# The causal mask of a decoder layer's attention: from a TensorE product to an addition on VectorE

## The chip, the cores and the metric

The kernel runs on one core of a Trainium2 chip. The metric is device time in microseconds (us); before the change it is 997.43 us, the median of three runs (995.61 to 999.0). The core has five engines that work side by side and meet only through semaphores: TensorE (PE in the profile, its weight loads PEld), VectorE (DVE), ScalarE (ACT), GpSimd (POOL) and SyncE (SP), which issues the DMAs.

## The reference

A decoder layer on 8 sequences of 256 tokens with 512 features: causal self-attention (16 heads of 32 features, 4 key heads), causal cross-attention to a context, and a feed-forward part, each with a residual and a layer norm. The part that matters is the same in both attentions:

```python
att = jnp.einsum('bhqd,bhkd->bhqk', q, k) * scale
causal = jnp.tril(jnp.ones((T, T), dtype=bool))
att = jnp.where(causal[None, None], att, -jnp.inf)
att = jax.nn.softmax(att, axis=-1)
y = jnp.einsum('bhqk,bhkd->bhqd', att, v)
```

## The kernel before

The attentions fill the first 525 us or so of the span; after them come the preparation of the feed-forward weights and the feed-forward part, which the change does not touch. The attentions are 16 **turns** (8 sequences of self-attention, then 8 of cross-attention), a turn has four **steps**, and a step handles one group of four heads. So there are 64 groups. A group's scores lie in three PSUM banks, its **units**: A (bank 0) has the first 128 queries against the first 128 keys for four heads, B and C (banks 1 and 2) have the last 128 queries against all 256 keys for two heads each.

Each step overlaps three groups. TensorE (`scores`, `transposes`, `outputs`) computes the scores of group i, transposes the probabilities of group i-1, multiplies those of group i-2 with the values, and then does one to three **fillers**: projections for this and the next turn (`sv`, `sq`, `sk` in self-attention, `cv`, `cq`, `ck`, `x1t` in cross-attention, `wo` and `wout` for the output). VectorE (`step` in its body) takes the maxima of group i (`maxima`), copies two transposed tiles of group i-1 with the reciprocals and the output of group i-2 between them (`probT_tile`, `reciprocals`, `output`), and then does its share of the fillers: the low halves of projections (`lo`, L710), or residual, statistics and normalisation (L777 to L787). ScalarE (`step` in its body) copies the first transposed tile (L668), does the exponentials of the three units with their sums (L678), and then its share of the fillers (L629, L633).

The order on each engine is written out by hand. What ties the engines together: TensorE may write unit u of the next group only when ScalarE has finished the exponentials of that unit (s_exp), the exponentials of a unit wait for its maxima (s_max), and the fillers alternate between banks 3 and 4, so that each filler on TensorE waits until the one before the last has been drained by VectorE or ScalarE.

The mask before: ahead of the scores of a unit, TensorE multiplies a 128x128 identity with a bf16 tile of zeros and -1e30 (L893 for unit A, 512 columns; L898 for B and C, 256 columns), which opens the accumulation in the bank; the score products then add to it. VectorE reads the bank once with one max-reduction for each unit (L736), negated.

Of the kernel before, what the change touches and what calls it, by code (L numbers as in the profile page):

```python
# [26 lines left out]
BF16 = mybir.dt.bfloat16  # L27
ALU = mybir.AluOpType
ACT = mybir.ActivationFunctionType
AX = mybir.AxisListType  # L30
# [305 lines left out]
def attention_phase(nc, ctx, sb, sem, A, banks, x2, ident, s_const, s_passed):  # L336
# [27 lines left out]
    mv = sb(ctx, "mv", [P, TT, 2])  # L364
    rstd = sb(ctx, "rstd", [P, TT, 2])
    half = sb(ctx, "half", [P, 1])
    ident16 = sb(ctx, "ident16", [P, P], BF16)
    mask16 = sb(ctx, "mask16", [P, HG, P], BF16)
    W_RING = 4
    wraw = sb(ctx, "wraw", [P, W_RING, D])  # L370

# [76 lines left out]
    with nc.Block() as block:  # L448
# [92 lines left out]
        @block.gpsimd  # L541
        def _(g):
            g.memset(ident[:, :], 0.0).then_inc(s_const, 1)
            g.memset(ident16[:, :], 0.0).then_inc(s_const, 1)
            g.memset(mask16[:, :, :], 0.0).then_inc(s_const, 1)
            g.memset(half[:, :], -0.5).then_inc(s_const, 1)
            g.wait_ge(s_const, 4)
            for m in (ident, ident16):
                g.affine_select(out=m[:, :], in_=m[:, :], compare_op=ALU.not_equal, fill=1.0, base=0,
                                pattern=[[-1, P]], channel_multiplier=1).then_inc(s_const, 1)  # L550

            g.affine_select(out=mask16[:, :, :], in_=mask16[:, :, :], compare_op=ALU.is_ge, fill=MASKED, base=0,
                            pattern=[[0, HG], [-1, P]], channel_multiplier=1).then_inc(s_const, 1)

            def split(hi, lo, raw, s_h, s_l, n):
                g.tensor_scalar(hi, raw, 1.0, 1.0, ALU.mult, ALU.mult).then_inc(s_h, 1)
# [54 lines left out]
        def _(s):  # L611
# [51 lines left out]
            def body(t):  # L663
                def step(i):
                    if t.turned(i):
                        s.wait_ge(s_T, t.groups(i - 2, U, 1))
                        bank = banks[T_BANKS[(U * (i - 1)) % 2]]
                        s.activation(probT[:, (i - 1) % 2, :, 0:P], bank[:, :].rearrange("p (j q) -> p j q", j=HG), ACT.Copy).then_inc(s_cpA, 1)  # L668
                    if not t.scored(i):
                        return  # L670
                    for u in range(U):
                        if u and t.turned(i):
                            s.wait_ge(s_T, t.groups(i - 2, U, u + 1))
                        s.wait_ge(s_max, t.groups(i - 1, U, u + 1))
                        heads = range(HG) if u == 0 else range(2 * (u - 1), 2 * u)
                        width, qt = (P, 0) if u == 0 else (S, 1)
                        for c, j in enumerate(heads):
                            ins = s.activation(prob[:, u, c * width:(c + 1) * width], banks[u][:, c * width:(c + 1) * width], ACT.Exp,  # L678
                                               bias=nmax[:, i % 2, qt, j:j + 1], accum_out=den[:, i % 2, qt, j:j + 1])
                        ins.then_inc(s_exp, 1)  # L680

                for i in range(t.steps()):
                    step(i)
                    weights(*split_at(t, i, True))
                    for name in t.fillers(i):
                        projection(t, name)
                    if t is first_cross and i == 2:
                        pr.wait_full(s, t, ("wo", TT - 1))
                    weights(*split_at(t, i, False))
# [4 lines left out]
        def _(v):  # L694
# [35 lines left out]

            def body(t):
                def maxima(i, u):
                    v.wait_ge(s_S, t.groups(i - 1, U, u + 1))
                    width, qt = (P, 0) if u == 0 else (S, 1)
                    heads = slice(0, HG) if u == 0 else slice(2 * (u - 1), 2 * u)
                    v.tensor_reduce(nmax[:, i % 2, qt, heads], banks[u][:, :].rearrange("p (j k) -> p j k", k=width), AX.X, ALU.max, negate=True).then_inc(s_max, 1)  # L736

                def probT_tile(i, u):
                    v.wait_ge(s_T, t.groups(i - 1, U, u + 1))
# [68 lines left out]
        def _(t_):  # L808
# [62 lines left out]
                t_.wait_ge(s_wlo, KEYS if name[0] == "sk" else QUERIES)  # L871
                projection(pro, name)
            t_.wait_ge(s_wlo, VALUES)
            t_.wait_ge(s_const, 7)

            def body(t):
                def scores(i):
# [10 lines left out]
                    for u in range(U):  # L888
                        bank = banks[u]
                        if t.turned(i):  # L890
                            t_.wait_ge(s_exp, t.groups(i - 2, U, u + 1))
                        if u == 0:
                            t_.matmul(bank[:, :].rearrange("p (j k) -> p j k", j=HG), ident16[:, :], mask16[:, :, :], start=True, stop=False, skip_group_check=True)  # L893
                            for j in range(HG):
                                ins = t_.matmul(bank[:, j * P:(j + 1) * P], qh[:, j, 0:P], kh[:, j, 0:P], start=False, stop=j == HG - 1, skip_group_check=True)  # L895
                        else:
                            diag = bank[:, :].rearrange("p (j c k) -> p j c k", j=2, c=2)[:, :, 1, :]
                            t_.matmul(diag, ident16[:, :], mask16[:, 0:2, :], start=True, stop=False, skip_group_check=True)  # L898
                            for c in (0, 1):
                                j = 2 * (u - 1) + c  # L900
                                ins = t_.matmul(bank[:, c * S:(c + 1) * S], qh[:, j, P:S], kh[:, j, :], start=False, stop=c == 1, skip_group_check=True)
                        ins.then_inc(s_S, 1)

                def transposes(i, u):
# [754 lines left out]
```

## Time and profile before

| what | value |
|---|---|
| median of 3 runs | 997.43 us |
| the profiled execution, its own time | 1000.47 us |
| its span | 998.7 us |
| PE, DVE, ACT, POOL busy | 914.9, 682.4, 526.4, 431.6 us |
| mean granted TensorE clock | 0.971 of full speed |
| chain that ended last | PE 25% of the span, DVE 5%, issue 1% |

An engine's busy time is an average over stages with different limits, and busy PE is not PE at its peak, since its instructions overlap. The time of a turn is read from the stretches between the first weight load of one turn's scores and that of the next.

### The profile page before, as it was taken

To read this page: it belongs to the slowest core of one execution; us is meant where nothing else is said; L and a number is where in the kernel's file an instruction comes from. 1 tells how busy PE (TensorE), PEld (TensorE's weight loads), DVE (VectorE), ACT (ScalarE), POOL (GpSimd) and SP (SyncE) were. 2 spreads that over 40 slices of the span, in tenths; PEclk is the share of its full clock that TensorE was granted. 3 is DMA by queue.
4 is the path that set the end of the run, shared out by engine and by line. 5 is a ranking of instruction groups with operands and counts; after the bars stand their busy time and mean duration, and the time that the engine had idled before them with its cause. 6 is when DMAs were issued, how large, how long until landed. Compare 5 with 4: busy or idle time off the path is not lost. (4 is left out here: it accounts for less than half of the span.)

```text
span 998.7 us, 19666 instructions
## 1 busy us (share of the span) xinstructions
PE 914.9 (92%) x6030; PEld 757.6 (76%) x6092; DVE 682.4 (68%) x1240; ACT 526.4 (53%) x1640; POOL 431.6 (43%) x603
## 2 busy tenths in 40 slices
PE   4899999999988999999995897989999999999993
PEld 4788888888767888888884665667778778778773
DVE  3667766777767777777774688693657657657466
ACT  3656555565557556766561433435564564564461
POOL 0233233342222222322222587970565565566466
PEclk8999999999999999999997898999999999999998
DMA  5313322334445535354420765541101101000001
GB/s 164 125 66 122 106 79 89 105 105 152 118 132 144 136 82 141 111 137 106 109 80 0 236 223 196 190 147 64 43 1 43 42 0 42 0 0 35 8 1 42
DMA packets 67043, 92.96 MB, mean 93 GB/s; under 512 B 7217, under 2 KB 41009, under 8 KB 66609
## 3 DMA queue, kind: packets, MB, share of 16 engines
q1 hardware_dynamic: 66992, 92.34, 29.8%
q8 instruction: 25, 0.41, 0.2%
q14 instruction: 26, 0.20, 0.1%
HBM read 39.89 MB, written 4.19 MB: 44 GB/s over the span
## 5 line engine op out<-in xcount | busy, mean ns | idle before, releaser
L678 ACT ACTIVATE prob<-bank,nmax 128x128 f32<-128x128 f32 (+1 forms) x512 | 207.0, 435 | 18.1 <-DVE nmax L736 17.7
L161 PE MATMUL bank<-w_ffn,hT 128*128 128x512 f32 x768 | 193.1, 403 | 0.0
L161 PEld LDWEIGHTS bank<-w_ffn,hT 128*128 128x128 f32 x768 | 141.6, 190 | 31.1 <-POOL hT L1372 0.2
L566 POOL TENSOR_SCALAR rwide<-rden 128x256 f32<-128x256 f32 x64 | 26.0, 406 | 255.7 <-DVE rden L745 255.7
L161 PE MATMUL bank<-xT,w_att 128*128 128x256 f32 x864 | 119.2, 290 | 12.8 <-DVE w_att L702 10.1
L736 DVE TENSOR_REDUCE nmax<-bank 128x2 f32<-128x512 f32 (+1 forms) x192 | 120.7, 683 | 13.7 <-PE bank L895 13.7
L161 PEld LDWEIGHTS bank<-xT,w_att 128*128 128x128 f32 x864 | 113.3, 196 | 16.5 <-DVE xT L725 7.3
L161 PE MATMUL bank<-tile 128*128 128x512 f32 x384 | 100.4, 416 | 19.8 <-DVE tile L1183 19.8
L678 ACT ACTIVATION_READ_ACCUMULATOR prob<-bank,nmax 128x1 f32 x512 | 113.9, 223 | 0.0
L913 PE MATMUL bank<-ident,prob 128*128 128x128 f32 x768 | 105.9, 274 | 0.8 <-ACT prob L678 0.4
L1444 ACT ACTIVATE ht<-bank,cols 128x128 f32<-128x128 f32 x192 | 72.2, 457 | 64.4 <-PE bank L1581 64.4
L161 PEld LDWEIGHTS bank<-tile 128*128 128x128 f32 x384 | 73.3, 197 | 42.5 <-DVE tile L1183 18.5
L161 PE MATMUL bank<-w_att,oT 128*128 128x512 f32 x384 | 97.7, 405 | 2.6 <-POOL oT L558 2.5
L913 PEld LDWEIGHTS bank<-ident,prob 128*128 128x128 f32 x768 | 88.5, 142 | 1.3 <-ACT prob L678 0.6
L161 PE MATMUL bank<-x2T,w_ffn 128*128 128x512 f32 x384 | 88.5, 391 | 1.0 <-POOLq L113 1.0
L1501 DVE TENSOR_TENSOR y<-bank,stage_bias 128x512 f32<-128x512 f32 x64 | 44.1, 690 | 64.1 <-PE bank L161 64.1
L741 DVE COPY probT<-bank 128x512 f32<-128x512 f32 x128 | 87.2, 681 | 1.1 <-PE bank L913 1.1
L161 PEld LDWEIGHTS bank<-x2T,w_ffn 128*128 128x128 f32 x384 | 72.0, 188 | 16.9 <-POOLq L113 1.4
L161 PEld LDWEIGHTS bank<-w_att,oT 128*128 128x128 f32 x384 | 71.6, 193 | 17.3 <-issue 3.2
L1372 POOL TENSOR_TENSOR hT<-ht,hT 128x512 fp32r<-128x512 f32 x48 | 67.2, 1399 | 38.1 <-ACT hT L1449 38.0
L668 ACT ACTIVATE probT<-bank 128x512 f32<-128x512 f32 x64 | 38.2, 597 | 85.7 <-PE bank L913 85.7
L1183 DVE TENSOR_TENSOR tile<-raw,tile 128x1024 fp32r<-128x1024 f32 x32 | 51.6, 1622 | 21.0 <-ACT tile L1100 20.7
(125 smaller groups left out, 1557.7 us busy)
## 6 DMA issues: line engine op xcount, KB each, us to landing
q<-stage SPq DMA_DIRECT2D x192, 128.0 KB, 2.3
k<-kstage SPq DMA_DIRECT2D x48, 256.0 KB, 3.6
raw<-in_ent_wT SPq DMA_DIRECT2D x32, 256.0 KB, 3.2
raw<-in_ent_pw SPq DMA_DIRECT2D x32, 256.0 KB, 3.7
xT_raw<-in_xT SPq DMA_DIRECT2D x8, 512.0 KB, 4.4
xres<-in_x SPq DMA_DIRECT2D x8, 512.0 KB, 3.6
xb<-x SPq DMA_DIRECT2D x8, 512.0 KB, 4.4
aux<-in_path_w SPq DMA_DIRECT2D x8, 512.0 KB, 3.5
```

The lines of the kernel that those rows point to most:

```text
L161: ins = t.matmul(out, lhs(a, k), rhs(b, k), start=first and n == 0 and m == 0, stop=last and n == len(kts) - 1 and m == 2, skip_group_chec ...
L566: g.tensor_scalar(rwide[:, i % 2, :, :].rearrange("p t (j d) -> p t j d", j=HG), src, 1.0, 1.0, ALU.mult, ALU.mult).then_inc(s_wide, 1)
L668: s.activation(probT[:, (i - 1) % 2, :, 0:P], bank[:, :].rearrange("p (j q) -> p j q", j=HG), ACT.Copy).then_inc(s_cpA, 1)
L678: ins = s.activation(prob[:, u, c * width:(c + 1) * width], banks[u][:, c * width:(c + 1) * width], ACT.Exp, bias=nmax[:, i % 2, qt, j:j + ...
L736: v.tensor_reduce(nmax[:, i % 2, qt, heads], banks[u][:, :].rearrange("p (j k) -> p j k", k=width), AX.X, ALU.max, negate=True).then_inc(s ...
L741: v.tensor_copy(probT[:, i % 2, 2 * (u - 1):2 * u, P:PW], bank[:, :].rearrange("p (j q) -> p j q", j=2)).then_inc(s_cpB, 1)
L913: ins = t_.transpose(bank[:, c * P:(c + 1) * P], prob[:, u, c * P:(c + 1) * P], ident[:, :])
L1183: v.tensor_tensor(tile[:, kt % HR, 1, :, :], raw[:, kt % R, :, :], tile[:, kt % HR, 0, :, :].bitcast(F32), ALU.subtract).then_inc(s_lo, 1)
L1372: g.tensor_tensor(hT[:, 1, :, i * P:(i + 1) * P], ht[:, u % HT, :, :], hT[:, 0, :, i * P:(i + 1) * P].bitcast(F32), ALU.subtract).then_inc ...
L1444: ins = s.activation(ht[:, u % HT, c, :], bank[:, c * P:(c + 1) * P], ACT.Identity, bias=shift(u // BT, c), scale=gain(u // BT, c))
L1501: k.drain(("mm", u), v.tensor_tensor(y[:, i, :], banks[plan.bank(("mm", u))][:, :], bias[:, s_, :], ALU.add))
```

## The change

TensorE no longer multiplies the mask; the first score product of a unit opens the accumulation. VectorE adds the mask while it looks for the maxima: `tensor_tensor_reduce` reads a head's scores from the bank and the mask from SBUF (a tile of 128x256 floats: zeros for the first 128 keys, the triangle for the last), writes the negated sum back in place, and keeps the minimum of what it wrote as the bias of the exponential. ScalarE then takes the exponential with scale -1. One instruction handles one head of 128 or 256 keys, where one max-reduction handled a whole unit of 512 columns. The wait ahead of each unit is now an instruction of its own (`wait_alone`).

```diff
@@ VectorE
                 def maxima(i, u):
-                    v.wait_ge(s_S, t.groups(i - 1, U, u + 1))
+                    wait_alone(v, s_S, t.groups(i - 1, U, u + 1), s_passed)
                     width, qt = (P, 0) if u == 0 else (S, 1)
-                    heads = slice(0, HG) if u == 0 else slice(2 * (u - 1), 2 * u)
-                    v.tensor_reduce(nmax[:, i % 2, qt, heads], banks[u][:, :].rearrange("p (j k) -> p j k", k=width), AX.X, ALU.max, negate=True).then_inc(s_max, 1)
+                    for c, j in enumerate(range(HG) if u == 0 else range(2 * (u - 1), 2 * u)):
+                        scored = banks[u][:, c * width:(c + 1) * width]
+                        ins = v.tensor_tensor_reduce(scored, scored, mask[:, S - width:S], scale=-1.0, scalar=3e38, op0=ALU.add, op1=ALU.min,
+                                                     accum_out=nmax[:, i % 2, qt, j:j + 1])
+                    ins.then_inc(s_max, 1)
@@ ScalarE
-                                               bias=nmax[:, i % 2, qt, j:j + 1], accum_out=den[:, i % 2, qt, j:j + 1])
+                                               scale=-1.0, bias=nmax[:, i % 2, qt, j:j + 1], accum_out=den[:, i % 2, qt, j:j + 1])
@@ TensorE
-                        if u == 0:
-                            t_.matmul(bank[:, :].rearrange("p (j k) -> p j k", j=HG), ident16[:, :], mask16[:, :, :], start=True, stop=False, skip_group_check=True)
-                            for j in range(HG):
-                                ins = t_.matmul(bank[:, j * P:(j + 1) * P], qh[:, j, 0:P], kh[:, j, 0:P], start=False, stop=j == HG - 1, skip_group_check=True)
-                        else:
-                            diag = bank[:, :].rearrange("p (j c k) -> p j c k", j=2, c=2)[:, :, 1, :]
-                            t_.matmul(diag, ident16[:, :], mask16[:, 0:2, :], start=True, stop=False, skip_group_check=True)
-                            for c in (0, 1):
-                                j = 2 * (u - 1) + c
-                                ins = t_.matmul(bank[:, c * S:(c + 1) * S], qh[:, j, P:S], kh[:, j, :], start=False, stop=c == 1, skip_group_check=True)
+                        width, at = (P, 0) if u == 0 else (S, P)
+                        heads = list(range(HG) if u == 0 else range(2 * (u - 1), 2 * u))
+                        for c, j in enumerate(heads):
+                            ins = t_.matmul(bank[:, c * width:(c + 1) * width], qh[:, j, at:at + P], kh[:, j, 0:width], start=c == 0, stop=c == len(heads) - 1, skip_group_check=True)
...
```

On GpSimd two small tiles of constants are no longer made before the first scores.

TensorE, the scores of one group before (bank0 is unit A, bank1 and bank2 are B and C; k3 and q3 are the stacked keys and queries):

```order
L893 MATMUL bank0<-mask16,ident16 128x512 [waits s_exp,s_qst2]
L895 MATMUL bank0<-k3,q3 128x128 x4
L898 MATMUL bank1<-mask16,ident16 128x2x128 [waits s_exp]
L901 MATMUL bank1<-k3,q3 128x256 x2
L898 MATMUL bank2<-mask16,ident16 128x2x128 [waits s_exp]
L901 MATMUL bank2<-k3,q3 128x256 x2
```

TensorE, the same place after the change:

```order
L895 MATMUL bank0<-k3,q3 128x128 [waits s_exp,s_qst2]
L895 MATMUL bank0<-k3,q3 128x128 x3
L895 MATMUL bank1<-k3,q3 128x256 [waits s_exp]
L895 MATMUL bank1<-k3,q3 128x256
L895 MATMUL bank2<-k3,q3 128x256 [waits s_exp]
L895 MATMUL bank2<-k3,q3 128x256
```

The three mask products are gone, and the waits stand at the first score product of each unit; nothing else moves.

VectorE, from the last filler of one self-attention step to the first copy of the next, before:

```order
L710 SCALAR_TENSOR_TENSOR stage<-bank4,stage 128x256 [waits s1_hi]
L733 REGISTER_ALU
L736 TENSOR_REDUCE nmax<-bank0 128x4 [waits s_S]
L733 REGISTER_ALU
L736 TENSOR_REDUCE nmax<-bank1 128x2 [waits s_S]
L733 REGISTER_ALU
L736 TENSOR_REDUCE nmax<-bank2 128x2 [waits s_S]
L741 COPY probT<-bank6 128x2x256 [waits s_T]
```

VectorE, the beginning of the same place after the change, units A and B (an ISA row that names a bank is the new operation, the ISA row with nmax alone behind it reads out the minimum that it kept):

```order
L707 SCALAR_TENSOR_TENSOR stage<-bank4,stage 128x256 [waits s1_hi]
L152 REGISTER_ALU
L734 ISA bank0,nmax<-bank0,mask 128x128 [waits s_S]
L734 ISA nmax 128x1
L734 ISA bank0,nmax<-bank0,mask 128x128
L734 ISA nmax 128x1
L734 ISA bank0,nmax<-bank0,mask 128x128
L734 ISA nmax 128x1
L734 ISA bank0,nmax<-bank0,mask 128x128
L734 ISA nmax 128x1
L152 REGISTER_ALU
L734 ISA bank1,nmax<-bank1,mask 128x256 [waits s_S]
```

Where three instructions stood for a group, sixteen stand now: eight that work on a head and eight that read out a minimum. Everything behind them on VectorE keeps its place.

## Rows read from the trace of the kernel before

**Rows 1.** Windows: a self-attention turn, the passage to cross-attention, a cross-attention turn
```profile
core 0: us, PE busy (x) PEld busy (x) DVE busy (x) ACT busy (x) POOL busy (x), PEclk, DMA share, GB/s
143.61:174.27 30.66, 30.66 (x270) 27.04 (x273) 21.79 (x46) 17.62 (x75) 11.17 (x18) 1.00 0.28 98
242.13:316.00 73.87, 65.62 (x530) 55.20 (x538) 54.66 (x107) 45.23 (x167) 18.14 (x37) 0.98 0.55 151
404.25:436.11 31.86, 30.70 (x260) 26.27 (x263) 24.01 (x49) 20.05 (x78) 8.86 (x18) 1.00 0.44 119
```

**Rows 2.** Timeline of TensorE's weight loads, a self step: start, length, operation
```profile
153.91 1.42 PEld L161 LDWEIGHTS bank<-w_att,xT 128*128 128x128 f32 x12
155.25 1.50 PEld L161 LDWEIGHTS bank<-xT,w_att 128*128 128x128 f32 x12
156.79 0.10 PEld L893 LDWEIGHTS bank<-mask,ident 128*128 128x128 bf16 x1
...
157.42 0.10 PEld L898 LDWEIGHTS bank<-mask,ident 128*128 128x128 bf16 x1
...
157.78 0.10 PEld L898 LDWEIGHTS bank<-mask,ident 128*128 128x128 bf16 x1
```

**Rows 3.** Groups of VectorE by line and shape: busy us, mean ns, idle before
```profile
L736 DVE TENSOR_REDUCE nmax<-bank 128x2 f32<-128x512 f32 x128 | 82.1, 682 | 0.0
L755 DVE TENSOR_TENSOR o<-bank,rT 128x256 f32<-128x256 f32 x64 | 27.2, 424 | 3.3
```

**Rows 4.** Timeline of VectorE in step 0 of a self turn
```profile
176.50 1.89 DVE L736 TENSOR_REDUCE nmax<-bank 128x4 f32<-128x512 f32 x3
```

**Rows 5.** Timeline of ScalarE in the same step
```profile
177.23 0.37 ACT L678 ACTIVATE prob<-bank,nmax 128x128 f32<-128x128 f32 x1 [0.37 <-DVE nmax L736]
...
177.59 0.36 ACT L678 ACTIVATE prob<-bank,nmax 128x128 f32<-128x128 f32 x1
...
179.51 0.50 ACT L678 ACTIVATE prob<-bank,nmax 128x256 f32<-128x256 f32 x1
...
179.96 0.51 ACT L678 ACTIVATE prob<-bank,nmax 128x256 f32<-128x256 f32 x1
180.32 0.24 ACT L678 ACTIVATION_READ_ACCUMULATOR prob<-bank,nmax 128x1 f32 x1
```

**Rows 6.** Timeline of weight loads: unit C of the step behind it
```profile
181.86 0.10 PEld L898 LDWEIGHTS bank<-mask,ident 128*128 128x128 bf16 x1
```

**Rows 7.** Waits of the cross turn 404.25 to 436.11: total us, times, longest
```profile
PEld bank L866 <- DVE stage L710: 1.0, 1, 1.0
...
PEld bank L161 <- ACT cv L633: 0.6, 1, 0.6
```

**Rows 8.** Timeline of VectorE in that cross turn, steps 0 and 2
```profile
406.20 1.88 DVE L736 TENSOR_REDUCE nmax<-bank 128x4 f32<-128x512 f32 x3
...
420.11 1.88 DVE L736 TENSOR_REDUCE nmax<-bank 128x4 f32<-128x512 f32 x3
...
422.50 0.19 DVE L745 RECIPROCAL rden<-den 128x8 f32<-128x8 f32 x1
422.61 0.37 DVE L751 COPY rT<-bank 128x256 f32<-128x256 f32 x1
...
423.36 0.68 DVE L741 COPY probT<-bank 128x512 f32<-128x512 f32 x1
424.99 0.69 DVE L710 SCALAR_TENSOR_TENSOR kstage<-bank,kstage 128x512 fp32r<-128x512 f32 x1 [0.95 <-ACT kstage L629]
```

**Rows 9.** Timeline of ScalarE in step 0 of that turn
```profile
406.92 0.37 ACT L678 ACTIVATE prob<-bank,nmax 128x128 f32<-128x128 f32 x1
...
410.09 0.64 ACT L633 ACTIVATE cv<-bank 128x512 f32<-128x512 f32 x1
```

**Rows 10.** Timeline of weight loads in that turn, steps 0 and 2
```profile
410.78 0.53 PEld L161 LDWEIGHTS bank<-w_att,ctxT 128*128 128x128 f32 x3 [0.62 <-ACT cv L633]
...
425.74 1.61 PEld L161 LDWEIGHTS bank<-xT,w_att 128*128 128x128 f32 x12
```

More of the change, by code:

```diff
@@ L366, in attention_phase @@
     half = sb(ctx, "half", [P, 1])
-    ident16 = sb(ctx, "ident16", [P, P], BF16)
-    mask16 = sb(ctx, "mask16", [P, HG, P], BF16)
+    mask = sb(ctx, "mask", [P, S])
     W_RING = 4
@@ L543, in _ @@
             g.memset(ident[:, :], 0.0).then_inc(s_const, 1)
-            g.memset(ident16[:, :], 0.0).then_inc(s_const, 1)
-            g.memset(mask16[:, :, :], 0.0).then_inc(s_const, 1)
+            g.memset(mask[:, :], 0.0).then_inc(s_const, 1)
             g.memset(half[:, :], -0.5).then_inc(s_const, 1)
[L547 to L553, printed above, removed]
+            g.wait_ge(s_const, 3)
+            g.affine_select(out=ident[:, :], in_=ident[:, :], compare_op=ALU.not_equal, fill=1.0, base=0,
+                            pattern=[[-1, P]], channel_multiplier=1).then_inc(s_const, 1)
+            g.affine_select(out=mask[:, P:S], in_=mask[:, P:S], compare_op=ALU.is_ge, fill=MASKED, base=0,
+                            pattern=[[-1, P]], channel_multiplier=1).then_inc(s_const, 1)
             def split(hi, lo, raw, s_h, s_l, n):
@@ L873, in _ @@
             t_.wait_ge(s_wlo, VALUES)
-            t_.wait_ge(s_const, 7)
+            t_.wait_ge(s_const, 5)
             def body(t):
```

## The prediction

> **What bounds the kernel now.** I read the busy shares first: PE 92% of the span, DVE 68%. That average hides what matters here, so next I cut the attentions into turns with the windows view. In a self-attention turn TensorE is busy in all of its 30.66 us, and VectorE in 21.79 [rows 1]. In a cross-attention turn TensorE has 30.70 us of work in 31.86, VectorE 24.01 [rows 1]. So self-attention goes by TensorE's work, and in cross-attention TensorE already waits. The waits of the cross turn say for whom: once for VectorE's low half of a projection, once for ScalarE's copy of cv, 1.0 and 0.6 us [rows 7]. Both stand at the end of the same chain: scores, maxima on VectorE, exponentials on ScalarE, the fillers' copies, TensorE's next filler. Then the timelines of single steps, to see where that chain is tight.
>
> **What TensorE saves.** The mask products are overlapped with loads, so I take spacings and not lengths. From the mask's weight load of unit B to that of unit C is 157.42 to 157.78, 0.36 us, for a mask product and two score products of 256 columns [rows 2]. Twelve products of that width in the filler take 155.25 to 156.79, 0.128 each, so two take 0.257, and the mask costs 0.10. Unit A takes 156.79 to 157.42, 0.63; four products of 128 columns cost four times (155.25 - 153.91) / 12 = 0.112, so 0.45, and the mask 0.18. A group saves 0.18 + 0.10 + 0.10 = 0.39 us (rounded up), a turn 1.56, all 64 groups 25 us. That is the whole possible gain, if nothing else becomes late.
>
> **What VectorE pays.** Removed: three reductions of 512 columns, 682 ns long [rows 3], but overlapping: three take 1.89 [rows 4], so one starts 0.605 after the other and 0.077 of each length is hidden. VectorE is held 1.8 us. Added: four instructions on 128 and four on 256 columns, and behind each a read-out. The trace has no such instruction, and none in which VectorE writes a bank.
> - The nearest row of the work itself: two tensors, one from a bank, 256 columns, 424 ns [rows 3]. The slope between it and the 512-column reduction is 258 ns for 256 columns, so 128 columns are 295 ns long. With 0.077 hidden: 0.218 and 0.347 apart.
> - The nearest row of a read-out: a reciprocal of 8 elements holds the engine 0.11 (422.50 to 422.61) [rows 8]. Then the group costs 4 x 0.328 + 4 x 0.457 = 3.14 us.
> - The nearest row of such a pair is ScalarE's exponential with its sum: pairs start 0.36 apart at 128 columns, 0.45 at 256 [rows 5]. Stretched to VectorE's slope (1.01 ns a column against (450 - 360) / 128 = 0.70) that is 0.40 and 0.53, 3.7 us a group; unstretched it is 3.24.
> - Lower end: the read-outs hide entirely, 2.26. Upper end: nothing overlaps and a read-out is 0.19 long, 4 x 0.485 + 4 x 0.614 = 4.40; if reading and writing one bank also halved the rate, 3.14 + 0.13 x 4 + 0.26 x 4 = 4.70.
>
> I take 3.3, near the first two prices: +1.5 us of VectorE for each group. Unit A, which ScalarE waits for first, is ready 1.44 us after the start in place of 0.68, B and C follow 0.97 us apart, faster than the exponentials of a unit need (four at 0.36), so only A delays them: 0.76 us.
>
> The Trainium skill, "Vector Engine (DVE) Microarchitecture Reference", section "Measured stream behaviour on trn2", gives 1.04 ns a column and about 75 ns fixed for each instruction, programs of several micro-operations included. An estimate from that page would be 0.21 and 0.34 for the work and 0.08 for a read-out, 2.8 us a group. The trace agrees on the slope (1.01) and the fixed part (0.605 - 0.516 = 0.09) for built-in operations; for this one it shows nothing. This speaks for the first rival below.
>
> **What it does in self-attention.** VectorE's 21.79 us become 27.8, below TensorE's new 29.1, so the sum does not decide, the order in the step does. In step 0 VectorE comes late to the maxima, since it first normalises for the turn before: it starts at 176.50 [rows 4], and ScalarE already waits for it 0.37 [rows 5]. That start hangs on VectorE's own work in step 3 and stays. The exponentials start 0.76 later, at 177.99, and end at 180.32 + 0.24 + 0.76 = 181.32. TensorE needs that for unit C of the next group, now at 181.86 [rows 6]; by its own work it will be there 0.39 (step before) + 0.39 + 0.28 (masks of A and B) = 1.06 earlier, 180.80. So it waits 0.5. The other three steps start their maxima early enough, or are long enough (two hold an output projection); I allow another 0.2. A turn: -1.56 + 0.7 = -0.86.
>
> **In cross-attention.** Step 0: maxima at 406.20 [rows 8], exponentials at 406.92, the copy of cv at 410.09 [rows 9], for which TensorE waits until 410.78 [rows 10]. The exponentials come 0.76 later and so does everything in this chain; TensorE's saving lies inside its wait. Since the fillers ahead end up to 0.15 earlier, I count +0.6. Step 1: its maxima wait for the scores, which come sooner; -0.1. Step 2: maxima at 420.11; the group holds VectorE 3.3, then the copies, reciprocal and output 423.96 - 421.90 = 2.06 (423.36 + 0.68 - 0.08 is their end [rows 8], 420.11 + 1.79 their start). So it is free at 425.5 for the low half of kstage, which now starts at 424.99 [rows 8]; TensorE's next filler, now just in time at 425.74 [rows 10], comes 0.5 later. Step 3 is hardly touched. A turn: +1.0.
>
> **Elsewhere.** The passage between the attentions (242 to 316) has VectorE at 54.66 of 73.87 us with the splitting of the cross weights [rows 1]; ten groups there bring it 15 us more. Where it is the one waited for (I count three steps) that is +1.5 each, less 0.39 in the seven others: +2. The constants on GpSimd and the sign of the exponential cost nothing: they lie beside DMAs, or are a field of the instruction.
>
> **The sum.** Seven self turns x -0.86 = -6.0; seven cross turns x +1.0 = +7.0 (one of each kind falls into the start or the passage); passage +2. Together +3. On the profiled execution, 1000.47, that is 1003.5. This execution stands 3.04 above the median of the runs, so 1000.5.
>
> **Rivals.**
> 1. TensorE's gain wins. If the group costs VectorE 2.8, A is ready 1.2 after the start: the exponentials are 0.5 later. Self turns then lose only some 0.4 of their 1.56 (-1.2, seven: -8.4), cross turns are about even (+0.1), the passage 0: -8, 989. At 2.26 it would be -20 (978). For it: TensorE's full 30.66 of 30.66. Against: VectorE's late start in step 0. Chance 0.30.
> 2. VectorE becomes the bound of both attentions. From about 3.9 us a group its work, 21.79 - 3 x 4 x 0.68 + 4 x 3.9 = 29.2, passes TensorE's 29.1 in self turns. At 4.4 it has 31.2 us and the 1.3 us or so of waits that stay: 32.5, +1.9 a turn; in cross turns 24.01 - 8.2 + 17.6 + 1.3 = 34.7, +2.9; with +8 in the passage +42, 1039. At 4.7 it would be 1055. The place is the same maxima, the price the pair of instructions. For it: ScalarE's pairs, stretched, give 3.7. Against: every VectorE row that follows another overlaps it. Chance 0.20, of which half beyond 1030.
> 3. The change does not free TensorE: the mask's products might fill time in which the stacked keys' loads could not run anyway. Then the spacings stay, and only VectorE's lateness is left: +15, 1012. The 0.36 against 0.257 speaks against it. Chance 0.05.
>
> My forecast (3.1 to 3.7 us a group) has 0.45, and its own range is 994 to 1015: above 3.3 each 0.1 us a group is worth about 3.5 us over the groups, in late maxima and late fillers, below it less, since TensorE's own work takes over.
>
> **Chances.** What a measurement can tell from no change is 0.3%, 3 us: below 994.4 is faster, above 1000.4 slower. Faster: rival 1 nearly whole, 0.27, and 0.02 of the forecast. Same: 0.23 of the forecast and 0.03 of rival 1. Slower: 0.20 of the forecast, rivals 2 and 3: 0.45. The range 984 to 1032 leaves out what lies beyond 2.5 us and 4.2 us a group.
>
> **What will show it.** TensorE: no rows with mask; the spacing of unit B 0.26 in place of 0.36, unit A 0.45. VectorE: 512 new instructions with 512 read-outs; from the first of a group to the copy behind it 3.3 us (2.8 for rival 1, over 3.9 for rival 2). Self turns 29.8 us long, with waits of TensorE for ScalarE's exponentials of some 0.5 in step 0; cross turns 32.9, with the waits for cv and kstage grown. The prediction is wrong if VectorE's rows come out under 3 or over 3.7 us a group, or if VectorE starts its maxima of step 0 earlier than now, so that self turns keep the whole 1.56.

## The result

| kernel | median of runs, us | lowest to highest | against before |
|---|---|---|---|
| before (4 runs of the same chip) | 998.11 | 995.61 to 999.0 | 1 |
| after (4 runs) | 987.66 | 985.95 to 989.78 | 0.990, 95% interval 0.987 to 0.9931 |

The change makes the kernel 1.0% faster. The forecast was 1000.5 us, no change or a little slower. The profiled execution of after took 986.26 us, its span 984.4.

**Where the time went.** Each group has one reciprocal on VectorE, 64 in all. I cut both traces at the 5th, 29th, 37th and 61st: six self turns, the passage, six cross turns (all groups of the same kind in both). Windows of before, columns as in [rows 1]:

```profile
61.67:247.81 186.14, 186.14 (x1631) 164.45 (x1654) 131.38 (x273) 107.09 (x456) 67.00 (x108) 1.00 0.31 103
247.81:319.21 71.40, 63.15 (x509) 52.73 (x516) 53.63 (x106) 43.88 (x163) 17.76 (x36) 0.98 0.52 142
319.21:510.41 191.20, 184.23 (x1549) 157.63 (x1574) 144.03 (x290) 120.29 (x470) 53.12 (x108) 1.00 0.43 116
```

The same windows of after:

```profile
59.67:235.85 176.18, 176.12 (x1578) 156.77 (x1578) 146.46 (x585) 107.27 (x453) 67.00 (x108) 1.00 0.33 109
235.85:308.27 72.42, 60.08 (x477) 50.47 (x479) 58.98 (x210) 43.71 (x162) 17.75 (x36) 0.96 0.49 138
308.27:498.50 190.23, 177.48 (x1522) 151.81 (x1515) 160.22 (x601) 122.12 (x474) 53.19 (x108) 1.00 0.44 117
```

Self-attention gives 9.96 us (1.66 a turn, all that TensorE saves); the passage takes 1.02 back; cross-attention gives only 0.97 (0.16 a turn). What is left of the 14.3 us between the two spans lies ahead of the 5th reciprocal (2.0) and between the 61st and the last (0.8), where seven changed groups stand, and behind the attentions (1.6), in code that the change does not touch; the runs of one kernel spread by 2 to 6 us. In the passage the granted clock is also lower, 0.96 against 0.98.

**What the group costs.** VectorE in step 0 of a self turn of after, against [rows 4]:

```profile
167.80 0.30 DVE L734 CUSTOM_DVE_ANT_0 bank<-bank,mask 128x128 f32<-128x128 f32 x1
168.01 0.14 DVE L734 DVE_READ_ACCUMULATOR2_ANT nmax<- 128x1 f32 x1
168.01 0.33 DVE L734 CUSTOM_DVE_ANT_0 bank<-bank,mask 128x128 f32<-128x128 f32 x1
168.26 0.14 DVE L734 DVE_READ_ACCUMULATOR2_ANT nmax<- 128x1 f32 x1
...
169.14 0.14 DVE L734 DVE_READ_ACCUMULATOR2_ANT nmax<- 128x1 f32 x1
169.14 0.46 DVE L734 CUSTOM_DVE_ANT_0 bank<-bank,mask 128x256 f32<-128x256 f32 x1
169.52 0.14 DVE L734 DVE_READ_ACCUMULATOR2_ANT nmax<- 128x1 f32 x1
...
170.29 0.68 DVE L741 COPY probT<-bank 128x512 f32<-128x512 f32 x1
```

A read-out has the same start as the next head's work: 140 ns long, it costs little. The first head's work, with no read-out beside it, is followed after 0.21 us, the next ones after 0.25: 0.04 for the read-out. So heads start 0.25 apart at 128 columns and 0.38 at 256, and the copy behind the group starts 170.29 - 167.80 = 2.49 us after its first instruction. So the group costs 2.5 us, not 3.3. ScalarE's first exponential of that step:

```profile
168.93 0.37 ACT L675 ACTIVATE prob<-bank,nmax 128x128 f32<-128x128 f32 x1 [1.40 <-DVE nmax L734]
```

That is 1.13 after the maxima's start, against 177.23 - 176.50 = 0.73 before [rows 4, 5]: A is 0.40 later, not 0.76. Among the groups of VectorE by line and shape, as in [rows 3], the read-outs are:

```profile
L734 DVE DVE_READ_ACCUMULATOR2_ANT nmax<- 128x1 f32 x512 | 71.5, 140 | 0.0
```

They are 71.5 us in the sum, and at 0.04 each some 20 us of VectorE's time: the busy time of overlapping instructions is no price.

**TensorE.** The scores of one self step, weight loads of after, against [rows 2]:

```profile
157.69 1.00 PEld L895 LDWEIGHTS bank<-k,q 96*128 96x128 f32 x8
158.63 0.47 PEld L907 LDWEIGHTS bank<-ident,prob 128*128 128x128 f32 x4
```

0.94 us from the first load to the load behind the segment. The whole self turn shrinks by 1.66, 0.41 a group; 0.39 was forecast.

**Waits.** TensorE's and ScalarE's waits in the cross window 319.21 to 510.41 of before (total us, times, longest):

```profile
PEld bank L866 <- DVE stage L710: 5.9, 6, 1.0
...
PEld bank L161 <- ACT cv L633: 3.7, 6, 0.6
...
ACT prob L678 <- DVE nmax L736: 2.1, 6, 0.4
```

and in the window 308.27 to 498.50 of after:

```profile
ACT prob L675 <- DVE nmax L734: 12.6, 18, 0.9
...
PEld bank L161 <- ACT cv L630: 8.9, 6, 1.5
...
PEld bank L866 <- DVE stage L707: 5.7, 6, 1.0
...
PEld bank L161 <- DVE kstage L707: 3.4, 6, 0.6
```

TensorE waits 18.0 us instead of 9.6. Of the 6 x 1.66 = 10.0 us that it saves in six turns, 8.4 come back as waits: 5.2 more for ScalarE's copy of cv, 3.4 for VectorE's low half of kstage, 0.2 less for stage. That is where the gain of cross-attention went. The rest of the window agrees: 191.20 - 10.0 + 8.4 = 189.6, measured 190.23.

Not all of it is VectorE's price. The same cross window of the kernel without any mask, whose VectorE does what it did before (experiment 1), has

```profile
PEld bank L161 <- ACT cv L633: 6.4, 6, 1.1
PEld bank L866 <- DVE stage L710: 5.6, 6, 1.0
...
PEld bank L161 <- DVE kstage L710: 0.5, 3, 0.2
```

so 2.9 of the 8.4 us come back only because TensorE is sooner at copies that are not, and 5.5 by VectorE's longer group (cv 2.5, kstage 2.9).

### The profile page after: what moved, and what is told of

Its sections match the earlier page's. It is cut to its first block and busy times, and to the rows that moved or that the text cites. A ratio compares the mean times of both kernels' runs of the same rounds, so it can differ in the third digit from the quotient of the medians.

```text
span 984.4 us, 20365 instructions
## 1 busy us (share of the span) xinstructions
PE 891.6 (91%) x5900; PEld 739.3 (75%) x5900; DVE 724.3 (74%) x2072; ACT 528.6 (54%) x1640; POOL 430.6 (44%) x601
## 5 line engine op out<-in xcount | busy, mean ns | idle before, releaser
L734 DVE CUSTOM_DVE_ANT_0 bank<-bank,mask 128x128 f32<-128x128 f32 (+1 forms) x512 | 164.1, 392 | 10.8 <-PE bank L895 10.5
L161 PE MATMUL bank<-xT,w_att 128*128 128x256 f32 x864 | 120.8, 293 | 15.4 <-DVE w_att L699 10.5
L675 ACT ACTIVATION_READ_ACCUMULATOR prob<-bank,nmax 128x1 f32 x512 | 111.6, 218 | 0.0
L1438 ACT ACTIVATE ht<-bank,cols 128x128 f32<-128x128 f32 x192 | 72.3, 457 | 64.2 <-PE bank L1575 64.2
L895 PE MATMUL bank<-k,q 96*128 96x128 f32 (+1 forms) x512 | 73.5, 286 | 5.1 <-DMA q<-stage 3.4
L895 PEld LDWEIGHTS bank<-k,q 96*128 96x128 f32 x512 | 66.3, 196 | 8.0 <-DVE w_att L699 2.5
```

Of the source, the lines that this page charges most:

```text
L161: ins = t.matmul(out, lhs(a, k), rhs(b, k), start=first and n == 0 and m == 0, stop=last and n == len(kts) - 1 and m == 2, skip_group_chec ...
L734: ins = v.tensor_tensor_reduce(scored, scored, mask[:, S - width:S], scale=-1.0, scalar=3e38, op0=ALU.add, op1=ALU.min, accum_out=nmax[:, ...
L895: ins = t_.matmul(bank[:, c * width:(c + 1) * width], qh[:, j, at:at + P], kh[:, j, 0:width], start=c == 0, stop=c == len(heads) - 1, skip ...
L1438: ins = s.activation(ht[:, u % HT, c, :], bank[:, c * P:(c + 1) * P], ACT.Identity, bias=shift(u // BT, c), scale=gain(u // BT, c))
```

## The experiments

The kernel before took 998.2 us beside experiments 1 to 3, 997.9 beside 4, 6 and 7, and 997.2 beside 5, 8 and 9; differences from before are taken from these. "Group" is the spacing from the first instruction of a group's maxima to the copy behind it; the windows are those between the same reciprocals.

| kernel | group, us | time, us | ratio to before, 95% | self turn | passage | cross turn |
|---|---|---|---|---|---|---|
| before | 1.80 | 998 | 1 | 31.02 | 71.4 | 31.87 |
| no mask at all | 1.80 | 978.9 | 0.9795 to 0.9836 | 29.27 | 71.0 | 30.64 |
| one instruction a unit | 1.90 | 981.0 | 0.9823 to 0.9853 | 29.27 | 72.3 | 30.94 |
| A stays on TensorE | 2.1 | 989.8 | 0.990 to 0.993 | 30.23 | 71.9 | 31.40 |
| after | 2.49 | 987.7 | 0.987 to 0.9931 | 29.36 | 72.4 | 31.71 |
| mask on both engines | 2.49 | 1005.4 | 1.0041 to 1.0085 | 31.08 | 72.6 | 32.44 |
| 0.8 us idle work behind C | 3.3 | 1005.1 | 1.0064 to 1.0099 | 30.02 | 74.7 | 32.39 |
| 0.8 us idle work, spread | 3.2 | 1002.9 | 1.0024 to 1.006 | 30.10 | 76.8 | 32.57 |
| 0.8 us idle work ahead of A | 3.3 | 1021.1 | 1.0213 to 1.0257 | 30.46 | 78.9 | 34.78 |
| one small copy a head | 2.7 | 1018.2 | 1.0195 to 1.0233 | 31.09 | 74.3 | 34.12 |
| two small copies a head | 3.3 | 1034.6 | 1.0352 to 1.039 | 32.46 | 76.9 | 35.20 |
| normalisation later | 2.5 | 983.8 | 0.9843 to 0.9872 | 29.31 | 71.9 | 31.51 |
| one instruction a unit, normalisation later | 1.9 | 975.8 | 0.9766 to 0.9805 | 29.29 | 70.9 | 30.56 |

**1. TensorE's gain by itself.** The kernel before, without any mask (it leaves the causal mask out):

```diff
-                            t_.matmul(bank[:, :].rearrange(...), ident16[:, :], mask16[:, :, :], start=True, ...)
                             ...
-                                ins = t_.matmul(bank[:, j * P:(j + 1) * P], ..., start=False, ...)
+                            ins = t_.matmul(bank[:, c * width:(c + 1) * width], ..., start=c == 0, ...)
```

> The kernel before without the mask products on TensorE; VectorE keeps its three max-reductions for a group, so the attention is not causal here. It gives TensorE's saving alone. By my theory (the mask's products cost TensorE 0.39 to 0.43 us a group; VectorE's later maxima gave part of it back in the changed kernel) self turns come to 30.66 - 4 x 0.42 = 29.0 us, cross turns, bound by the chain through the exponentials, to some 31.0; the time is 16 to 22 us under the kernel before, 976 to 982, and 6 to 12 under the changed kernel. By the rival theory (VectorE's dearer maxima cost nothing at all, the whole change is TensorE's saving) it equals the changed kernel, 987 to 988.

Measured 978.9 us (978.07 to 981.66), 19.3 under before. That is what TensorE's saving is worth while VectorE does what it did: 1.75 us a self turn, 1.23 a cross turn. The passage, with eight groups, gains only 0.4 (its granted clock is 0.95 here). So cross turns and passage give part of the saving back before VectorE does anything more. Rival 3 falls.

**2. VectorE's price by itself.** The changed kernel, and TensorE does its mask products too (the mask is applied twice):

> The changed kernel with TensorE's mask products put back: VectorE adds the mask a second time in place and takes the minima head by head. It gives VectorE's price alone: 0.7 us more of VectorE for a group, unit A ready some 0.45 us later. My theory: the self turns have slack and stay within 0.2 us of 30.66 (a wait for the exponentials of unit C just begins to show), the cross turns become 0.6 to 1.0 us longer (32.5 to 32.9), together +5 to +10 us, 1003 to 1008. Rival (VectorE's lateness is hidden everywhere): within 0.3% of the kernel before.

Measured 1005.42 us (1000.87 to 1006.73), 7.2 over before and 17.8 over after. In the profile most of it is in cross-attention (+0.57 a turn) and the passage (+1.2); a self turn does not see it (+0.06). The two parts nearly add up, -19.3 + 7.2 = -12.1, measured -10.5. VectorE's price is higher once TensorE is quick: a cross turn pays 0.57 here, and 31.71 - 30.64 = 1.07 with the mask off TensorE.

**3. One and two more small operations a head.**

```diff
                     for c, j in enumerate(...):
+                        v.tensor_copy(idle[:, 4 * u + c:4 * u + c + 1], half[:, :])
+                        v.tensor_copy(idle[:, ...], half[:, :])     # the second, in the second run
                         ins = v.tensor_tensor_reduce(scored, scored, mask[:, S - width:S], ...)
```

> The changed kernel with one small copy on VectorE (one column, SBUF to SBUF) ahead of each head's instruction, eight for a group. If such an operation holds VectorE 0.08 to 0.11 us, a group costs VectorE 3.2 to 3.4 us, the price that the prediction took. If only that price was wrong and the steps from it to the time were right, the time is that of the prediction: 998 to 1003. If the steps were too dark as well, it stays clearly below: 988 to 994 (self turns under 29.5 us).

> The same with two small copies ahead of each head, sixteen for a group: VectorE 3.9 to 4.3 us a group. By the prediction's second rival VectorE's work then passes TensorE's in the self turns (over 30 us) and sets both kinds of turn: 1022 to 1040. If VectorE's queue hides more than that, under 1010.

Measured 1018.23 (1014.39 to 1020.17) and 1034.63 us (1033.77 to 1035.87). The first misses both of its ranges; the second lies in its range, but not for the reason expected. A copy holds the engine 0.07 us, and part of that hides: with one a head, heads start 0.28 and 0.41 apart and the group takes 2.7 us (3.2 to 3.4 was expected), with two it takes 3.3. VectorE, with one copy, at 128 and at 256 columns:

```profile
101.95 0.15 DVE L735 COPY idle<-half 128x1 f32<-128x1 f32 x1
102.02 0.29 DVE L736 CUSTOM_DVE_ANT_0 bank<-bank,mask 128x128 f32<-128x128 f32 x1
102.23 0.14 DVE L736 DVE_READ_ACCUMULATOR2_ANT nmax<- 128x1 f32 x1
102.23 0.15 DVE L735 COPY idle<-half 128x1 f32<-128x1 f32 x1
...
103.12 0.42 DVE L736 CUSTOM_DVE_ANT_0 bank<-bank,mask 128x256 f32<-128x256 f32 x1
103.46 0.14 DVE L736 DVE_READ_ACCUMULATOR2_ANT nmax<- 128x1 f32 x1
```

With a copy between them the work alone shows: 0.21 and 0.34 us to the row behind it.

But six times VectorE stands still for 2.3 to 2.8 us with nothing to wait for, and the step there is that much longer or twice that. Each attention has a loop of three passes of two turns (eight groups). The stops lie where the second and the third pass begin, once each in self-attention and twice each in cross-attention, and none lies where the first pass begins. Two of them:

```profile
113.18 0.15 DVE L735 COPY idle<-half 128x1 f32<-128x1 f32 x1 [2.81 <-issue]
...
377.97 0.15 DVE L735 COPY idle<-half 128x1 f32<-128x1 f32 x1 [2.27 <-issue]
```

The packets of the queue that brings instructions (packets, MB, share) show something of the kind: before, after, the next kernel (three more instructions a group) and this one (eight more):

```profile
q14 instruction: 26, 0.20, 0.1%
```
```profile
q14 instruction: 29, 0.24, 0.1%
```
```profile
q14 instruction: 30, 0.25, 0.1%
```
```profile
q14 instruction: 52, 0.42, 0.1%
```

The six stops are 15.5 us, of some 31 that this kernel stands over after. The granted clock is lower too, 0.97 in the self window and 0.96 in the cross window, 1.00 in both of after. So these two runs do not measure a price of time on VectorE, and reading them needed another experiment.

**4. The same time with few instructions.** The changed kernel, and one maximum over 192 columns of the mask tile for each unit, into a cell that nobody reads:

```diff
                     width, qt = (P, 0) if u == 0 else (S, 1)
+                    v.tensor_reduce(idle[:, u:u + 1], mask[:, 0:192], AX.X, ALU.max)
```

> The changed kernel with one instruction more for each unit: VectorE takes the maximum of 192 columns of the mask tile into a cell that nobody reads (three a group, 0.27 us each by the reductions' slope, 0.258 us for 256 columns and 0.09 fixed). It adds as much time to VectorE's group (2.48 + 0.8 = 3.3 us) as the 16 small copies did, with 3 instructions in place of 16. Theory (the long steps at every second turn of the runs with small copies come from the number of VectorE's instructions in the loop body, which must be fetched again when the loop jumps back; the time per group does the rest): no step is 3 us longer than its like, the instruction queue stays near the 29 packets of the changed kernel, self turns are about 29.8 us, cross turns 32.5 to 33.9, and the time is 1000 to 1012 us. Rival (the stalls come from VectorE's time itself, at a place where the two-turn loop ends): the steps at every second turn grow by 3 us or more again, and the time is 1020 us or more, as with two copies.

Measured 1002.91 us (999.05 to 1005.33). VectorE has no such stop. The window of its passage:

```profile
243.79:320.62 76.83, 62.95 (x483) 53.18 (x483) 64.24 (x234) 43.87 (x164) 18.18 (x36) 0.91 0.45 126
```

This is nearly the kernel that the prediction described: a group of 3.2 us. It stands 5.0 us over before; the forecast was 3 over. Had the group cost what I took it to, the forecast would have been near (by terms of which two were off in opposite ways, see below). And two small copies a head, at about the same group, take 32 us more. That comes with the number of instructions, not with the time on VectorE: 15.4 us are its six stops; its granted clock is 0.96 and 0.94 in the self and cross windows against 1.00 here, and how much of the rest is the clock's no run separates.

**5. Is it A's lateness, or the sum?** The prediction said that only A delays the exponentials. Two kernels with the same three idle maxima, all ahead of A's first instruction, or all behind C's last:

```diff
+                    for n in range(U if u == 0 else 0):        # ahead of A (the other: u == U - 1, behind C)
+                        v.tensor_reduce(idle[:, ...], mask[:, 0:192], AX.X, ALU.max)
```

> The changed kernel with three maxima of 192 columns of the mask tile into unread cells, all three ahead of unit A's first instruction: 0.8 us more VectorE a group, the same as with one ahead of each unit (1002.9 us), but A is ready 1.95 us after the start in place of 1.4. Theory (the lateness of A, and with it of all exponentials, is what costs; the sum of a group counts little while VectorE has idle time in a step): self turns over 30.5 us, cross turns over 32.8, 1006 to 1015 us. Rival (the sum of VectorE's work decides): as with one ahead of each unit, 1001 to 1005.

> The same three maxima, but behind unit C's last instruction, after ScalarE has been told that the group's minima are there: A is ready after 1.13 us as in the changed kernel, and the same sum of 3.3 us comes ahead of the copies of the transposed probabilities. Theory (A's lateness costs): self turns 29.4 to 29.7, cross turns 31.9 to 32.3 because their fillers on VectorE come later too, 990 to 996 us. Rival (the sum decides): 1001 to 1005.

Measured 1021.1 us (1017.5 to 1023.91) and 1005.07 (1002.92 to 1008.04). Both lie outside the ranges of the theory, that A's lateness is what costs. The first is dearer (1006 to 1015 was expected). The second refutes it: with A as early as in after, it costs as much as the spread kernel, which the theory excluded (990 to 996). The waits in its cross window, where after has cv 8.9, stage 5.7 and kstage 3.4:

```profile
PEld bank L161 <- ACT cv L631: 8.9, 6, 1.5
...
PEld bank L869 <- DVE stage L708: 8.5, 6, 1.5
...
PEld bank L161 <- DVE kstage L708: 5.4, 6, 0.9
```

cv is untouched: what this wait gains in other kernels is A's lateness. The 4.8 us more of stage and kstage are VectorE's own fillers behind the longer group: that is the sum. In self-attention the sum counts as well, by another way. TensorE's waits for exponentials in the self windows of after, of idle work behind C and of idle work spread:

```profile
PEld bank L895 <- ACT prob L675: 0.2, 1, 0.2
```
```profile
PEld bank L898 <- ACT prob L676: 2.3, 6, 0.6
```
```profile
PEld bank L897 <- ACT prob L676: 3.4, 7, 0.6
```

Behind C the exponentials follow their maxima as in after, but VectorE comes later to the maxima of step 0, 2.7 to 3.0 us behind TensorE's first load of that group in place of 2.3 to 2.6. That wait, and 1.4 us for the copies of the transposed probabilities, make a self turn 0.66 longer than in after; with the idle work spread it is 0.74.

So there are two paths, and each has its price. Ahead of A both are paid: cv 13.6, kstage 8.1 (stage 5.7), and TensorE's granted clock falls to 0.95 in the cross window (it is 1.00 in after), which is part of the 34.78. How much of the 1021 is the clock's, no run separates.

**6. A stays where it was**, in both attentions or in cross-attention alone (`moved` says whose mask VectorE adds):

```diff
+                        moved = u > 0                       # the other: u > 0 or t.own == "self"
+                        if not moved:
+                            t_.matmul(bank[...], ident16[:, :], mask16[...], start=True, stop=False, ...)
```

> The changed kernel, but unit A's mask stays a TensorE product and its maxima one reduction of 512 columns, as before the change; units B and C are as after it. TensorE keeps 0.20 to 0.25 of its 0.43 us a group; VectorE's group is 0.6 + 4 x 0.38 = 2.1 us in place of 2.48, and A is ready 0.7 us after the start in place of 1.13, as before the change. Theory (VectorE's price that counts is how late A is ready, not the sum): cross turns fall from 31.4 to 31.0 or so, self turns rise from 29.1 to 29.8, and the time is 986 to 991 us, no better than the change in full. Rival (the sum of the group is what counts): the same saving of 0.38 in every group shows in the cross turns' steps 2 and 3, and the time falls below 984.

> The changed kernel, but in cross-attention alone unit A's mask stays on TensorE with one reduction on VectorE; self-attention is wholly as after the change. If A's lateness is what cross turns pay (they gain 0.45 us of 1.6), they fall from 31.4 to about 31.0, seven of them and the passage by about 3 us: 984 to 986 us. Rival: TensorE's own 0.2 us a step comes back onto the path in the two steps that do not wait, and the time stays at 987 to 989.

Measured 989.78 (987.76 to 991.38), in its range, and 986.18 us (984.91 to 987.96), 0.2 above its range. Cross turns are 31.40 in both, self turns 30.23 where A's product stays, much as the theory had it. But both kernels also shorten the group (to 2.1 us; the wait for kstage is gone with that for cv down to 5.1), so they do not tell A's lateness from the sum. Over after the second is 1.5 us better, which these runs do not tell from nothing (after 985.95 to 989.78). Neither is clearly better than after: leaving a part of the mask returns to TensorE what TensorE has just been relieved of.

**7. The normalisation behind the next maxima** (so that VectorE reaches them sooner):

> The changed kernel, but VectorE normalises the finished residual (L787, 3 small operations of 512 columns) behind the first maxima of the next step in place of ahead of them. If VectorE's late start in the steps behind a normalisation is what keeps the exponentials late (the wait for the maxima there is 1.4 us in self turns and 0.4 in cross turns), the exponentials come 0.4 to 0.9 us earlier in those steps, TensorE's waits for them go, and the time is 982 to 986 us. Rival: the copies of the transposed probabilities, which now stand behind the normalisation, become as late as the maxima were, and the time is 987 to 992.

Measured 983.76 us (982.59 to 987.89), 3.9 under after, with ranges that overlap. A self turn stays at 29.31, since TensorE had hardly a wait left in it (0.2 us in six turns); the cross turns lose 0.2 and the last groups 1.1. The profiled execution is the slowest of its four, 987.89, so its windows do not add up to the gain. In experiment 9, beside experiment 8, they do better: the passage loses 1.45, a cross turn 0.38, the last groups 1.1.

**8. One instruction a unit.** What costs is columns plus a fixed part for each instruction: (0.38 - 0.25) / 128 = 1.0 ns a column, and 0.25 - 0.13 = 0.12 us fixed. Eight fixed parts become three when the heads of a unit share one minimum (a softmax is the same for any shift common to its row):

```diff
-                    for c, j in enumerate(range(HG) if u == 0 else range(2 * (u - 1), 2 * u)):
-                        scored = banks[u][:, c * width:(c + 1) * width]
-                        ins = v.tensor_tensor_reduce(scored, scored, mask[:, S - width:S], ..., accum_out=nmax[:, i % 2, qt, j:j + 1])
+                    scored = banks[u][:, :].rearrange("p (j k) -> p j k", j=n)
+                    masks = mask[:, S - width:S].rearrange("p (o k) -> p o k", o=1).broadcast_to([P, n, width])
+                    v.tensor_tensor_reduce(scored, scored, masks, ..., accum_out=nmax[:, i % 2, qt, 2 * max(u - 1, 0):2 * max(u - 1, 0) + 1])
```

(ScalarE's bias names the same shared cell.)

> The changed kernel, but one instruction for a whole unit in place of one for each head: the mask tile is repeated over the heads by a stride of zero, and the heads of a unit share the minimum over all of them as their bias (the softmax is the same for any shift that is common to a row). Three instructions and three read-outs a group in place of eight and eight. From the measured spacings, 0.25 us at 128 columns and 0.38 at 256 (1.0 ns a column and 0.12 fixed), 512 columns take 0.64 us, the group 1.9 to 2.0 in place of 2.48; A is ready 0.8 us after the start in place of 1.13. TensorE keeps its whole saving. Theory (VectorE's price per group decides what is left of TensorE's saving; at 1.8 us, with the mask left out, the time was 978.9): 979 to 983 us. Rival (the repeated mask or the three-dimensional view costs the operation its rate, 0.9 us or more a unit): a group of 2.7 us or more, 990 to 996 us.

Measured 980.96 us (980.19 to 982.44). VectorE, the same place as above; the group takes 160.10 - 158.20 = 1.90:

```profile
158.20 0.69 DVE L735 CUSTOM_DVE_ANT_1 bank<-bank,mask 128x512 f32<-128x512 f32 x1
158.81 0.14 DVE L735 DVE_READ_ACCUMULATOR2_ANT nmax<- 128x1 f32 x1
...
160.10 0.69 DVE L741 COPY probT<-bank 128x512 f32<-128x512 f32 x1
```

TensorE's waits in its cross window are 13.9 us in place of after's 18.0 (cv 6.8, stage 5.7, kstage 1.4).

It keeps 16.2 of the 19.3 us that leaving the mask out gains; its waits are near those of that kernel (12.5). What it gives up: a head whose scores all lie far below those of its unit's other heads would lose its exponentials to underflow, so it is for inputs of which that can be excluded.

**9. Both.**

> One instruction a unit as in the run beside it, and VectorE normalises the finished residual behind the next step's first maxima. Alone the later normalisation gave 983.8 against 987.7 of the changed kernel. Theory (both remove the same lateness, of the exponentials in the steps behind a normalisation): together 977 to 981, less than the sum of their gains. Rival (independent): 975 to 977. If the later normalisation only moves the wait to the copies of the transposed probabilities: no better than one instruction a unit alone.

Measured 975.79 us (972.79 to 977.61), ratio 0.9786 (0.9766 to 0.9805): the best version, 21 us under before and some 12 under the change as it was made. The later normalisation gives 5.2 us here and 3.9 alone, so nothing of its gain is lost, which speaks against the theory that the two remove the same lateness.

## Why the prediction was wrong

The step that failed is one term of "What VectorE pays": the read-out. The prediction's sum was 4 x 0.328 + 4 x 0.457 = 3.14, of which eight read-outs at 0.11 are 0.88 and the work is 2.26; it then went up to 3.3 by the likeness of ScalarE's pairs. Measured: heads 0.25 and 0.38 apart, and the work alone 0.21 and 0.34 (experiment 3), so a read-out costs 0.04. The group is 2.49, nearer my lower end of 2.26 than the 3.3. The 0.11 came from a reciprocal with a copy behind it, the step up to 3.3 from another engine's read-outs. Neither is this instruction: the row nearest in what it does was not the nearest in what it costs.

- **The work itself** held: two tensors, one from a bank, written back in place, 0.21 and 0.34 against 0.218 and 0.347. Writing the bank which it reads, one reason for the upper bound, costs nothing that these rows show.
- **TensorE's saving**, 0.39 a group, held (0.41).
- **Self turns**, forecast -0.86: by the prediction's own working the exponentials end at 181.32 with a lateness of 0.76, at 180.96 with the measured 0.40, and TensorE is there at 180.80: 0.16 of wait in place of 0.5. The scores of that step do take longer than 0.94 from first load to the load behind them, in two of the six turns (1.13 and 1.19):

```profile
171.42 1.19 PEld L895 LDWEIGHTS bank<-k,q 96*128 96x128 f32 x8
172.55 0.90 PEld L907 LDWEIGHTS bank<-ident,prob 128*128 128x128 f32 x8
```

  1.13, that is 0.19 of wait. With a group of 3.2 the self turns were -0.92 against before (30.10 to 31.02), and TensorE waited for the exponentials up to 0.6 about once a turn: the place and the size held, the input was wrong. One step of the working was wrong too, that VectorE's start in step 0 "hangs on VectorE's own work in step 3 and stays". That work holds a group itself, and the start moves with it (experiment 5): 0.66 of the 0.74 us that a self turn grows by come also with A early. That the wait came out near 0.5 is luck in part.
- **Cross turns**, forecast +1.0: the two waits named, cv and kstage, are the ones that grew. With 3.2 us the turn came out +0.70, with 2.49 -0.16.
- **The passage**, forecast +2: +1.0 in after, +5.4 in the kernel with 3.2. There the granted clock of the window was also lower, 0.91 against 0.98 before. With the idle work behind C it was 0.98, and the passage took +3.3. The term was too small, and the cross turns' too large: at 3.2 us, 7 x -0.92 + 7 x 0.70 + 5.4 = +3.9, where the prediction had +3. That the sum came so near is luck: the two errors nearly cancel.
- **"Only A delays them"** was wrong as a rule (experiment 5): VectorE's own work behind the group, its fillers and the start of its next maxima, is a second path of about the same weight.
- **The rivals.** Rival 1 is what happened; its 989 for 2.8 us and 978 for 2.26 put 2.49 at about 983, and 987.7 was measured. It gave back too little: what it had for 2.26 us, 978, takes a group of 1.80 and no mask at all (978.9), since a cross turn keeps 1.23 of the 1.66 us and the passage 0.4 of 3.3. Its ground was the estimate of 2.8 us by "Vector Engine (DVE) Microarchitecture Reference" of the Trainium skill, "Measured stream behaviour on trn2": the trace agrees on 1.0 ns a column; of the fixed 75 ns for each instruction it shows 0.08 for the work (0.21 - 0.13), which agrees, and 0.04 for the read-out, which is about half. That page's number stood nearer to the truth than each of my two analogies, and I had the trace's own check of it (0.09 fixed, 1.01 a column). Rivals 2 and 3 are excluded.

## What to carry to other kernels

Price an added instruction by spacing, and by the nearest row of the same engine's pipeline; a small follow-up instruction may cost far less than the shortest other one (here 0.04 us against 0.11). When work moves from the busiest engine to one that is 70 to 80% busy, list every step on which the second engine is late and split its price in two: what comes ahead of the first consumer, and what comes ahead of its own later work; behind C alone 0.8 us cost 18 us here, ahead of A, where both are paid, 34, a part of which is the clock's. And a saving on the busiest engine is worth little where that engine already waits: 0.41 us a group gave 19.3 us and not 26. Then cut the number of instructions before giving anything back: three instructions a group in place of eight kept 16.2 of the 19.3 us.

## What the runs showed of the hardware that was not expected

- The read-out of a kept minimum runs beside the next instruction: same start, 140 ns long, 0.04 us of VectorE's time. `tensor_tensor_reduce` in place in a PSUM bank costs 0.25, 0.38 and 0.64 us at 128, 256 and 512 columns, also where the second operand is repeated by a stride of zero.
- A loop body of VectorE may grow too long. At 16 instructions a group, and at 19, there was no sign of it; at 24 VectorE stood still for 2.3 to 2.8 us, once or twice where the second and the third pass of a two-turn loop begin and never where the first does, with nothing to wait for, and the packets of the instruction queue went from 29 to 52. That the code is fetched again when the loop jumps back fits all of this; no run shows it directly.
